# A two-layer mixture-of-experts block: routing in two halves, gates' last steps through PSUM, the rotary sum in TensorE

## What is computed

```python
h = layernorm(x) * (1 + ca) + sa                      # both layers
# layer 0 mixer: selective scan; layer 1 mixer: attention, 16 heads of 8,
q, k = h @ Wq.T + bq, h @ Wk.T + bk                   # 2048 tokens, layer 1
q = q * cos + rotate_half(q) * sin                    # k the same
x = x + ga * mixer(h)
h = layernorm(x) * (1 + cb) + sb
# layer 0 experts: top 2 of 8 by softmax(h @ Wr + br), each expert keeps at
# most cap = ceil(1.2 * 2048 / 8) pairs, those with the highest gate
rank = position among the pairs of that expert, by falling gate
y0 = sum over kept pairs of gate * (silu(h @ W1[e] + b1[e]) @ W2[e] + b2[e])
# layer 1 experts: top 2 of 8, weights divided by their sum, no cap, gelu
x = x + gb * y
```

## Time and profile before

| | us |
|---|---|
| median of three runs | 1249.47 (1246.38 to 1252.04) |
| profiled execution | 1248.94, of which the span is 1247.1 |
| PE busy | 1107.3 (89%) |
| DVE busy | 875.0 (70%) |
| ACT busy | 808.6 (65%) |
| POOL busy | 313.7 (25%) |
| chain of waits, by engine | PE 59%, no visible wait 11%, DVE 9%, ACT 7%, DMA 7%, POOL 6% |

### The profile page before, as it was taken

One profiled execution on the slowest core, in us unless ns is written; L12 is line 12 of the kernel. 1 busy time (PEld: TensorE's weight loads), 2 busy tenths in 40 slices (PEclk: granted clock), 3 DMA queues, 4 the chain that ended last, 5 costly groups with the idle time before them and its releaser, 6 DMA issues.

```text
span 1247.1 us, 21348 instructions
## 1 busy us (share of the span) xinstructions
PE 1107.3 (89%) x7774; PEld 533.4 (43%) x7774; DVE 875.0 (70%) x1621; ACT 808.6 (65%) x1211; POOL 313.7 (25%) x312
## 2 busy tenths in 40 slices
PE   8847779797985699999999999999999999988885
PEld 6412227697852123333333333333333332367885
DVE  2499985465049788888888888888888882263223
ACT  3653323275544578888988888889888889431222
POOL 0079850478735300000000000000000000005773
PEclk7969998799998789999999999999999999988997
DMA  3065610587542311101110011101110000006883
GB/s 102 1 181 196 198 57 34 170 278 216 160 154 95 100 47 37 33 5 36 36 37 14 25 37 36 33 5 36 36 37 9 25 4 4 3 34 246 282 263 135
DMA packets 50348, 107.17 MB, mean 86 GB/s; under 512 B 9796, under 2 KB 12132, under 8 KB 49860
## 3 DMA queue, kind: packets, MB, share of 16 engines
q1 hardware_dynamic: 44166, 93.89, 23.4%
q0 software_dynamic: 4992, 10.23, 2.7%
q10 hardware_dynamic: 1086, 1.68, 0.4%
HBM read 92.41 MB, written 12.94 MB: 84 GB/s over the span
## 4 chain that ended last, share of the span: by engine, by line
PE 59%; issue 11%; DVE 9%; ACT 7%; DMA 7%; POOL 6%; SPq 0%; ACTq 0%; DVEq 0%; POOLq 0%
PE psum L939 17%; PE psum L930 16%; PE psum L918 10%; ACT probs L1290 5%; DMA x_got<-xtok_dram,get_row 3%; PE psum L1045 3%; PE psum L1057 3%; POOL y_dram L1525 2%; PE psum L765 2%; DVE ssm_h L1692 1%; PE psum L743 1%; POOL x_got L1518 1%; PE psum L1035 1%; PE psum L756 1%; DMA y_in<-y_dram 1%
## 5 line engine op out<-in xcount | busy, mean ns | idle before, releaser
L1290 ACT ACTIVATE probs<-psum 128x1024 f32<-128x1024 f32 x512 | 495.9, 1022 | 51.6 <-PE psum L930 51.4
L1970 DVE TENSOR_REDUCE tile_max<-psum 128x1 f32<-128x512 f32 x720 | 466.6, 686 | 68.3 <-PE psum L918 62.5
L918 PE MATMUL psum<-k_stack,q_stack 64*128 64x512 bf16 x994 | 332.5, 386 | 16.4 <-DMA q_stack<-q_dram 13.8
L930 PE MATMUL psum<-q_stack,k_stack 64*128 64x512 bf16 x1024 | 284.6, 381 | 4.6 <-DMA q_stack<-shift_rows 0.9
L939 PE MATMUL psum<-probs,v_head 128*32 128x512 f32 x2048 | 272.7, 605 | 0.6 <-ACT probs L1290 0.6
L918 PEld LDWEIGHTS psum<-k_stack,q_stack 64*128 64x128 bf16 x994 | 89.7, 94 | 272.7 <-DVE tile_max L1970 120.7
L1491 POOL TENSOR_TENSOR max_parts<-row_max,no_shift 128x8 bf16<-128x8 f32 x32 | 6.4, 200 | 591.5 <-DVE row_max L1946 591.5
L930 PE MATMUL psum<-q_stack,k_ext 64*128 64x512 bf16 x512 | 144.3, 379 | 0.0
L930 PE MATMUL psum<-q_stack,ln_xc 64*128 64x512 bf16 x512 | 137.6, 376 | 0.0
L1518 POOL DMA_INDIRECT x_got<-xtok_dram,get_row x78 | 79.3, 1017 | 101.8 <-issue 60.1
L930 PEld LDWEIGHTS psum<-q_stack,k_stack 64*128 64x128 bf16 x1024 | 70.3, 94 | 53.4 <-ACT probs L1290 31.8
(11 more groups left out here) (272 smaller groups left out, 1324.8 us busy)
## 6 DMA issues: line engine op xcount, KB each, us to landing
w1r<-w SPq DMA_DIRECT2D x78, 256.0 KB, 4.0
w2r<-w SPq DMA_DIRECT2D x78, 256.0 KB, 3.9
ssm_b<-bc_dram SPq DMA_DIRECT2D x32, 512.0 KB, 4.4
k_stack<-k_dram SPq DMA_DIRECT2D x60, 120.0 KB
y_in<-y_dram SPq DMA_DIRECT2D x16, 256.0 KB, 5.3
q_stack<-q_dram SPq DMA_DIRECT2D x30, 96.0 KB
bc_p<-bc_dram SPq DMA_DIRECT2D x5, 512.0 KB, 5.5
k_stack<-k_dram SPq DMA_DIRECT2D x30, 80.0 KB
```

The costliest lines, as they stand in the source:

```text
L918: mm(bank, queries, k_stack[rows, u, keys:keys + C], start=True, stop=True).then_inc(s1_ps, 1)
L930: return mm(psum[:, 2 * slot + side, :], k[side_rows(side), kt * 128:(kt + 1) * 128], q_stack[side_rows(side), u, part, at:at + C], start= ...
L1290: f(probs[:, kt % 4, hf * HALF:(hf + 1) * HALF], banks(2 * slot, 2), ACT.Exp, scale=SCALE).then_inc(p_ready, 1)
L1970: v.tensor_reduce(top, bank, AX.X, ALU.max).then_inc(s1_read, 1)
```

## The change

Five places. The two `busy` calls ahead of the routed norms are gone. Routing is done in two halves of eight tiles: the logits of each half have a PSUM bank of their own, DVE starts on the first half during the norm's last chunk, and the number of small steps doubles while each covers 64 columns. ACT loads Exp's table right after the last Sqrt. `keep_capacity` works in chunks of 512 columns with the intermediate in PSUM bank 3; the pass that marks equal gates over all 2048 columns stays, and is done once more by chunk. In the rotary stage PE adds both products: the identity times q·cos, then the rotation times q·sin, into one bank; DVE multiplies by the cosine straight from the projection's bank, POOL by the sine, and ACT and DVE read the sum from PSUM. ACT keeps copies in SBUF of the two key chunks that POOL needs later.

```diff
-                busy(psum[:, 7, :], 10)
...
-                    i = mm(psum[:, 4, t * NE:(t + 1) * NE], normT[:, t * 128:(t + 1) * 128], router_w[layer],
+                    i = mm(psum[:, 4 + c // 2, t * NE:(t + 1) * NE], normT[:, t * 128:(t + 1) * 128], router_w[layer],
                            start=True, stop=True)
-                if c == NC - 1:
+                if c % 2:
...
+                        pe.wait_ge(cos_ready, m - 1)
...
+                def turn_pairs(m):
+
+                    pe.wait_ge(cos_ready, m + 1)
                     if m >= 2:
-                        pe.wait_ge(sin_ready, m - 1)
-                    mm(psum[:, 6 + m % 2, :], mat("rotate"), chunk(qkT[j], c), start=True, stop=True).then_inc(rot_ps, 1)
+                        pe.wait_ge(rest_ready, m - 1)
+                    mm(psum[:, 6 + m % 2, :], mat("ident"), rope_cos[:, m % 2, :], start=True, stop=False)
+                    pe.wait_ge(sin_ready, m + 1)
+                    mm(psum[:, 6 + m % 2, :], mat("rotate"), rope_sin[:, m % 2, :], start=False, stop=True).then_inc(roped, 1)
...
+                project(1)
...
-                    rotate(m)
+                    turn_pairs(m)
+                    if m + 2 < 2 * NC:
+                        project(m + 2)
...
-                busy(psum[:, 0, :], 10)
...
+                    if following is not None and c == NC - 1:
+                        table(following)
...
-                table(ACT.Exp)
-                act.wait_ge(shifted_ready, layer + 1)
-                f(rt["prob"][:], rt["logit"][:], ACT.Exp).then_inc(exp_ready, 1)
+                for hf in range(2):
+                    act.wait_ge(shifted_ready, 2 * layer + hf + 1)
+                    f(rt["prob"][:, half_tiles(hf), :], rt["logit"][:, half_tiles(hf), :], ACT.Exp).then_inc(exp_ready, 1)
...
+                    if (c, j) in APART_OF:
+                        f(chunk(qkT[j], c), psum[:, 6 + m % 2, :], ACT.Identity).then_inc(kept_ready, 1)
+                    f(chunk(qk_parts[j][:, 0, :], c), psum[:, 6 + m % 2, :], ACT.Identity).then_inc(hi_ready, 1)
...
                 raw(1)
                 for m in range(2 * NC + 1):
+                    if m < 2 * NC:
+                        hi(m)
                     if m + 2 < 2 * NC:
                         raw(m + 2)
-                    if m < 2 * NC:
-                        hi(m)
...
-                    g.tensor_tensor(rope_cos[:, m % 2, :], chunk(qkT[j], c), chunk(cosT, c), ALU.mult).then_inc(cos_ready, 1)
+                    g.tensor_tensor(rope_sin[:, m % 2, :], chunk(qkT[j], c), chunk(sinT, c), ALU.mult).then_inc(sin_ready, 1)
...
+                pool.wait_ge(kept_ready, len(APART_OF))
...
+                dve.wait_ge(exp_ready, 2 * layer + hf + 1)
+                step(v.tensor_reduce(rs["sum"][:, at], rt["prob"][:, at, :], AX.X, ALU.add))
+                step(v.reciprocal(rs["inv"][:, at], rs["sum"][:, at]))
+                step(v.tensor_tensor(rt["prob"][:, at, :], rt["prob"][:, at, :], wide(rs["inv"]), ALU.mult))
+
+                def best(src, top, n):
+                    step(v.tensor_reduce(rs[top][:, at], rt[src][:, at, :], AX.X, ALU.max))
+                    step(v.tensor_tensor(rt["eq"][:, at, :], rt[src][:, at, :], wide(rs[top]), ALU.is_equal))
+                    step(v.tensor_tensor(rt["eq"][:, at, :], rt["eq"][:, at, :], each(expert_no), ALU.mult))
+                    step(v.tensor_reduce(rs["no"][:, at], rt["eq"][:, at, :], AX.X, ALU.min))
+                    step(v.tensor_tensor(masks[:, n, at, :], wide(rs["no"]), each(expert_no), ALU.is_equal))
+
+                best("prob", "top1", 0)
+                if ahead is not None:
+                    ahead()
+                step(v.scalar_tensor_tensor(rt["rest"][:, at, :], masks[:, 0, at, :], -4.0, rt["prob"][:, at, :], ALU.mult, ALU.add))
+                best("rest", "top2", 1)
...
+                def shifted(hf):
+                    at = half_tiles(hf)
+                    logits = psum[:, 4 + hf, 0:TILES * NE].rearrange("p (t e) -> p t e", e=NE)[:, at, :]
+                    dve.wait_ge(logits_ready, 2 * layer + hf + 1)
+                    if layer == 0:
+                        step(v.tensor_tensor(rt["logit"][:, at, :], logits, router_b.unsqueeze(1).to_broadcast([128, TILES // 2, NE]), ALU.add))
+                    else:
+                        step(v.tensor_copy(rt["logit"][:, at, :], logits))
+                    step(v.tensor_reduce(rs["max"][:, at], rt["logit"][:, at, :], AX.X, ALU.max))
+                    v.tensor_tensor(rt["logit"][:, at, :], rt["logit"][:, at, :],
+                                    rs["max"][:, at].unsqueeze(2).to_broadcast([128, TILES // 2, NE]), ALU.subtract).then_inc(shifted_ready, 1)
+
+                shifted(0)
+                route(layer, 0, ahead=lambda: shifted(1))
+                route(layer, 1)
...
                 step(v.tensor_scalar(gate_eq[:], gates_rep[:], low, None, ALU.is_equal))
-
-                step(v.tensor_tensor_scan(gate_rank[:], gate_eq[:], gate_eq[:], 0.0, ALU.add, ALU.max))
-                step(v.scalar_tensor_tensor(gate_eq[:], gate_rank[:], thr_f["quota"][:], gate_eq[:], ALU.is_le, ALU.mult))
-                step(v.scalar_tensor_tensor(gate_eq[:], gates_rep[:], low, gate_eq[:], ALU.is_gt, ALU.add))
-                v.tensor_tensor(gate_valid[:], gates_rep[:], gate_eq[:], ALU.mult).then_inc(gates_step, 1)
+                for c in range(NC):
+                    gates, rank, kept = chunk(gates_rep, c), chunk(gate_rank, c), psum[:, 3, :]
+                    step(v.tensor_scalar(kept, gates, low, None, ALU.is_equal))
+                    step(v.tensor_tensor_scan(rank, kept, chunk(gate_eq, c), gate_rank[:, c * C - 1:c * C] if c else 0.0, ALU.add, ALU.max))
+                    step(v.scalar_tensor_tensor(kept, rank, thr_f["quota"][:], kept, ALU.is_le, ALU.mult))
+                    step(v.scalar_tensor_tensor(kept, gates, low, kept, ALU.is_gt, ALU.add))
+                    i = v.tensor_tensor(chunk(gate_valid, c), gates, kept, ALU.mult)
+                    if c + 1 < NC:
+                        step(i)
+                    else:
+                        i.then_inc(gates_step, 1)
...
+                def cosine(m):
                     c, j = PARTS[m]
-                    dve.wait_ge(rot_ps, m + 1)
-                    v.tensor_tensor(rope_sin[:, m % 2, :], psum[:, 6 + m % 2, :], chunk(sinT, c), ALU.mult).then_inc(sin_ready, 1)
-                    dve.wait_ge(sin_ready, m + 1)
-                    dve.wait_ge(cos_ready, m + 1)
-                    v.tensor_tensor(chunk(qkT[j], c), rope_cos[:, m % 2, :], rope_sin[:, m % 2, :], ALU.add).then_inc(roped, 1)
+                    dve.wait_ge(qk_raw, m + 1)
+                    if m >= 2:
+                        dve.wait_ge(roped, m - 1)
+                    v.scalar_tensor_tensor(rope_cos[:, m % 2, :], psum[:, 4 + m % 2, :], col(("bq", "bk")[j]), chunk(cosT, c),
+                                           ALU.add, ALU.mult).then_inc(cos_ready, 1)
...
-                    v.tensor_tensor(qk_rest[:, m % 2, :], chunk(qkT[j], c), chunk(qk_parts[j][:, 0, :], c), ALU.subtract).then_inc(rest_ready, 1)
+                    v.tensor_tensor(qk_rest[:, m % 2, :], psum[:, 6 + m % 2, :], chunk(qk_parts[j][:, 0, :], c), ALU.subtract).then_inc(rest_ready, 1)
...
+                for m in range(2 * NC + 3):
                     if m < 2 * NC:
-                        rope(m)
-                    if 0 <= m - 1 < 2 * NC:
-                        rest(m - 1)
-                    if 0 <= m - 2:
-                        low(m - 2)
+                        cosine(m)
+                    if 0 <= m - 2 < 2 * NC:
+                        rest(m - 2)
+                    if 0 <= m - 3:
+                        low(m - 3)
```

More of the change, by code:

```diff
@@ L130 @@
 PARTS = [(c, 1) for c in range(NC)] + [(c, 0) for c in range(NC)]
+APART_OF = ((0, 1), (1, 1))
 PLAIN, APART, JOINED = range(3)
@@ L1722, in step, with route, wide, each @@
                 dve.wait_ge(route_step, steps[0])
-            def wide(t):
-                return t[:].unsqueeze(2).to_broadcast([128, TILES, NE])
-            def each(t):
-                return t.unsqueeze(1).to_broadcast([128, TILES, NE])
+            def route(layer, hf, ahead=None):
+                at = half_tiles(hf)
+                def wide(t):
+                    return t[:, at].unsqueeze(2).to_broadcast([128, TILES // 2, NE])
+                def each(t):
+                    return t.unsqueeze(1).to_broadcast([128, TILES // 2, NE])
+                dve.wait_ge(exp_ready, 2 * layer + hf + 1)
[13 more added lines that the diff above has]
+                best("rest", "top2", 1)
             def place(layer):
-                logits = psum[:, 4, 0:TILES * NE].rearrange("p (t e) -> p t e", e=NE)
                 if layer == 0:
@@ L1735, in place @@
                     v.memset(ones_b[:], 1.0).then_inc(place_ready, 1)
-                    dve.wait_ge(logits_ready, 1)
```

(16 more changed lines are left out.)

25 lines of the change are left out of this document (8 added, 17 removed).

## The result

The changed kernel took 1238.15 us (median of six, 1230.44 to 1247.36) against 1250.76 for the kernel before; the ratio is 0.9888, 95% interval 0.9854 to 0.9922. Two later timings against the kernel before gave 0.9861 (0.9817 to 0.9904) and 0.9880 (0.9842 to 0.9918). So it is 1.1 to 1.4% faster, 12.6 us by the first medians; 13.75 were forecast.

A forecast was written before the change was run, and what follows sets the result against it. PE, busy 89%, was not the bound everywhere: in each changed place another engine or unread PE work set the end. Terms −4.3 + 1.4 − 7.15 − 3.7 = −13.75 gave 1235.5 us, range 1231 to 1242.5.

The forecast's parts named there:

- C: Gates' last steps in the expert blocks: POOL's four stretched transfers shrink from 11.06 to 3.91 us, −7.15, all on the chain.
- D: Rotary stage: PE sets 2.58 us a part and the first store comes at 394.9 against 398.60, −3.7 us.
- A: Routed norms: both runs of ten unread matmuls were on the chain; removing them gives 2 × 2.16, −4.3 us.
- signs of being wrong: POOL's transfers at 2 us or more, rotary sums at 3.3, PE's products at 1.7, or routed norms longer from first mean.
- rival 3: Routed norms: the clock falls earlier without the ten matmuls, some 2.5 us a norm, total 1240.7; chance 0.10.
- B: Routing in halves: 34 small steps in place of 17, +0.9 in layer 0 and +0.5 in layer 1, together +1.4 us.
- cover of 7 us: Gates: DVE's chain of twenty steps ends at 306.4, 7 us before the turn of the gates is wanted at 313.8.
- a second operand in SBUF makes the stall: Gates: chunk steps with at most one big SBUF operand leave POOL's transfers unstretched, as under the search; basis of −7.15 us.
- Rival 1: Gates: dense DVE passes as such stretch POOL's transfers, so that part gives 0, total 1242.9; chance 0.09.
- rival 2: Rotary stage: DVE or POOL still sets the pace as the last remainder collides with POOL's product, +0.7, total 1240.1; chance 0.20.
- The mis-sized step: End of the rotary stage: after the last rotation at 393.1, the first store waits for one piece of each kind, 394.9.
- Rival 4: Rotary stage at half clock: store at about 413, +14.5, total 1253.9; decides from 5.3 of eight parts; chance 0.03.

The follow-up runs named there:

- a_alone: The kernel before with only the two runs of ten unread matmuls taken away; ratio 0.9972 (0.9944 to 1.0000).
- b_alone: The kernel before with only the routing in halves, its bank and the table load; ratio 0.9996 (0.9970 to 1.0022).
- d_alone: The kernel before with only the rotary sum in TensorE; ratio 0.9921 (0.9892 to 0.9950).
- c_alone: The kernel before with only the gates' last steps in chunks through PSUM; ratio 0.9937 (0.9912 to 0.9962).
- all: The whole change against the kernel before, first timing; 1238.15 us, ratio 0.9888.
- all_third: The changed kernel unaltered, traced and timed a third time; 1236.54 us, ratio 0.9880 to the kernel before.
- norm_busy: The changed kernel with two unread matmuls added in the third and fourth part of each routed norm; ratio 0.9896 to the kernel before.
- gates_1024: The kernel before with the gates' last steps in two chunks of 1024 columns, intermediate in SBUF; ratio 1.0007.
- best: The changed kernel without the routing in halves and without the full marking pass; 1232.86 us, ratio 0.9861 to the kernel before.
- gates_sbuf: The kernel before with the gates' last steps in chunks of 512 columns, intermediate in SBUF instead of PSUM; ratio 0.9943.
- all_again: The changed kernel unaltered, run once more on a slower chip; 1280.32 us, ratio 0.9861 to the kernel before.

## Why the prediction was right, and where not

The total was right: 12.6 us of 13.75, and the three ratios make it 14 to 18, each with 4 to 6 either way. By the stages the terms are −3.6, +1.1, −5.6 and −5.5, −13.6 in all. That this lies so near the forecast is in part luck: C gave 1.5 us less on its path and D 1.8 more. The terms:

**A, −4.3.** Right: −2.16 a norm in a_alone, −1.81 a norm over all traces. In the first trace of the changed kernel the gain was eaten in both norms: from the first mean on they took 17.0 and 16.6 us, where before shows 14.22 twice. That is one of the prediction's own signs of being wrong, and what rival 3 describes. The later traces show that it isn't the ten: the clock falls with and without them, and costs 0.95 and 1.29 us a norm. Had only the pair of profiles been compared, the wrong story would have been told. What decides where the clock falls in an execution stays open.

**B, +1.4.** Right: `either` stands 9.69 behind the last product start, of which the 34 steps take 8.8 (204.69 to 213.50), with 0.32 idle for the trip to ACT. The cost by the stages is +1.1.

**C, −7.15.** The size of POOL's relief was right: under the chunk steps that replace the four passes no transfer is stretched. On the path it is −5.6 up to the turn of the gates (mean of before, a, b, d_alone 91.3; of c_alone, all, all_third and norm_busy 85.6). From the turn to the rotary stage the traces of before and gates_1024, a, b, d_alone take 49.2 on average, those four 52.3; one of them, norm_busy, has 56.0. PE's clock falls in these blocks in all of them, at different places, and whether C brings some of that isn't settled; c_alone (49.9) and best (49.2) have C's chunks without the longer stretch. DVE's chain of twenty steps took 17.6 us (291.44 to 309.03), not 16: the prediction took the old running sum's 4.42 for stretched by POOL and allowed a quarter at most 1.1, but a quarter takes 1.23 to 1.28 where no transfer is stretched. The cover of 7 us took that up. The cause was only half right. The step that said that a second operand in SBUF makes the stall is confirmed, but it left out the length of the pass. Without the transfer under the marking pass the excess is 7.15 before and 1.4 in gates_sbuf, so some 5.7 go by cutting the passes alone, with the operand left in SBUF, and 1.4 more by PSUM. The two traces are of different chips, and POOL had 12 transfers under the steps of gates_sbuf and 15 in c_alone, so the split is rough. Rival 1's passage, that dense DVE passes stall whatever their operands, is refuted by all seven PSUM traces. So is the inference of the Trainium skill, "SBUF — State Buffer", section "Who interferes with whom", that a two-operand pass leaves descriptor generation alone. Another sentence of that section of the Trainium skill says of DVE's two-port modes that whoever issues first has the shared pair for the whole instruction and the other fully blocks. gates_1024 and gates_sbuf show such a block, to the end of the one pass, for passes with two SBUF operands as well.

**D, −3.7.** Mechanism right, size too small: −5.5 (rotary 40.7 on average in the six traces without D, 35.2 in the eight with it). At one clock it is −6.0 (first projections at full clock: 40.2 and 34.2) or −5.9 (at half: 41.7 and 35.8). The last remainder takes 0.68 in all key parts, where it took 1.75 before, so rival 2 didn't come. The mis-sized step is the end: the store was to wait for two pieces on ACT behind the last rotation, 1.8 us. In all_third, at full clock throughout:

```profile
362.92 1.98 PE L871 MATMUL psum<-normT,mats 128*128 128x512 f32 x4 [0.78 <-DVE ln_xn L1629]
...
384.62 1.02 PE L880 MATMUL psum<-rope_sin,mats 128*128 128x512 f32 x2
385.48 3.73 PE L889 MATMUL psum<-mats,normT 128*128 128x128 f32 x32
```

```profile
385.68 0.60 ACT L1249 ACTIVATE q_parts<-psum 128x512 bf16<-128x512 f32 x1 [1.38 <-PE psum L880]
385.74 0.63 ACTq L570 DMA_DIRECT2D q_dram<-q_parts  x1
```

The last rotation ends at 385.48, 22.56 behind the start (23.1 forecast), and the store is issued 0.26 later, while ACT still works on a piece. In the code `store_q` waits only for the pieces of the first six parts, which are done by then (the sixth part's last remainder ends at 385.46), and stands in ACT's order behind the first piece of the eighth. Before, the chain shows it held by the sixth part's remainder:

```profile
396.97 1.61 DVE q_parts L1926
398.57 0.02 issue
398.60 0.63 ACTq L565
```

So it comes 22.8 behind the start, not 24.9; before it was 28.6. The store isn't what attention waits for any more either: the chain goes by the key's store and SP's queue of loads. Counted from the start of the stage, the last store of the key is issued 3.7 us earlier than before, and `q_negative` comes 5.1 earlier.

**Rival 4** was there in small: the first two projections ran at half clock in five of the eight traces with the new rotary stage (3.64 to 3.78 in place of 1.98), and the stage took 35.4 to 36.4 in them against 34.1 to 34.4 in the other three. The old stage did the same in b_alone and c_alone (3.78), so it doesn't come from D alone. That is 1 to 2 us, one part's worth, far from the 5.3 parts that the rival needed.

## What to carry to other kernels

Where one engine's instruction holds up another's, look at what the other loses: in these traces it was the rest of that one instruction. Then cut the long ones, even before thinking of where their operands lie, and take away the waiting party's last collisions afterwards. And where the clock or anything else varies from run to run, a pair of profiles shows a term only if its stage is cut out and read in several executions; here the first profile hid 4 us that the change does give.

## What the runs showed of the hardware that was not expected

One chip took 1296.25 us for the kernel that takes 1250 to 1252 on the others. For the same program nearly all of it is in the expert blocks, with their weights and gathers: 108.4 against 84.5 to 85.0 us from the first gather to the turn of the gates in layer 0, and 136.6 against 117.1 to 119.6 from the first gather to the end in layer 1, while from the second `q_negative` to the residual behind attention it took 667.6, and 667.2 on the other chips. An indirect transfer of POOL seems to need what a two-operand pass of DVE holds from about 0.12 us behind its start, an estimate (0.97 less 0.85): those that began 0.07 to 0.13 us before such a pass ended took 0.97 to 1.00, two that began 0.22 before it took 1.06.

The full marking pass acts in another way. Transfers that began 0.24 to 0.65 us into it ended 0.84 to 0.91 behind its end, as with the other passes. Those that began between 0.29 us ahead of it and 0.02 us into it ended 0.12 behind its end, as here in all_again, POOL and DVE:

```profile
303.55 1.51 POOL L1529 DMA_INDIRECT x_got<-xtok_dram,get_row  x1 [0.30 <-issue]
```

```profile
303.65 1.29 DVE L1914 TENSOR_SCALAR gate_eq<-h0T,thr_low 128x2048 f32<-128x2048 f32 x1
```

So this pass also stops a transfer that is already running, which a two-operand pass does not: in before the transfer from 290.73 ends at 295.56 under a pass that began at 294.80.
